# One attention kernel on one core: the shift of the scores summed by one matmul of stacked halves

## The reference

```python
q = jnp.einsum('bte,ef->btf', emb, Wq) + bq
k = jnp.einsum('bml,le->bme', latent, Wk) + bk
v = jnp.einsum('bml,le->bme', latent, Wv) + bv
w = jnp.einsum('bte,bme->btm', q, k) * scale        # scale = 1/sqrt(E)
w = jax.nn.softmax(w, axis=1)                       # over the tokens t
pred = jnp.einsum('btm,bme->bte', w, v)
x = pred + emb
return (x - mean(x)) * rsqrt(var(x) + EPS) * gamma + beta
```

## Time and profile before

| | |
|---|---|
| three runs | 143.15, 143.27 and 142.31 us, median 143.15 us |
| the profiled execution | 142.91 us |
| its span, first to last instruction | 141.2 us |
| mean granted TensorE clock | 0.994 of full speed |
| busy: TensorE, its weight loads, VectorE, ScalarE, GpSimd | 134.6, 130.4, 114.2, 79.0, 60.8 us |

### The profile page before, as it was taken

The page is one execution under the profiler, slowest core; times in us unless marked ns, Lnnn a source line. Parts: engine busy times, 40 slices in busy tenths (PEclk is TensorE's granted clock), DMA queues, the critical chain, the costliest instruction groups (busy, mean ns, idle before and its releaser), DMA issues.

```text
span 141.2 us, 2971 instructions
## 1 busy us (share of the span) xinstructions
PE 134.6 (95%) x1046; PEld 130.4 (92%) x1046; DVE 114.2 (81%) x221; ACT 79.0 (56%) x282; POOL 60.8 (43%) x61
## 2 busy tenths in 40 slices
PE   6999999999999999999999999999999999999940
PEld 6899999999998999999999999999999999999940
DVE  0479994996996769999999976878789976797983
ACT  4257088577276926466474829474747546386420
POOL 1000000027304590734848370629385644629791
PEclk9999999999999999999999999999999999999997
DMA  4999999956087495986998889796987987536314
GB/s 153 301 402 420 422 305 384 325 229 216 15 252 246 169 379 176 372 319 198 322 340 273 313 277 389 218 353 205 336 310 214 347 267 250 214 102 230 113 73 150
DMA packets 10814, 37.33 MB, mean 264 GB/s; under 512 B 1200, under 2 KB 1456, under 8 KB 10800
## 3 DMA queue, kind: packets, MB, share of 16 engines
q1 hardware_dynamic: 9424, 34.79, 71.0%
q10 hardware_dynamic: 1376, 2.36, 4.4%
HBM read 33.87 MB, written 3.28 MB: 263 GB/s over the span
## 4 chain that ended last, share of the span: by engine, by line
PE 89%; POOL 5%; issue 2%; ACT 1%; DVE 0%; POOLq 0%; DVEq 0%
PE ps_S L418 29%; PE ps_U L432 26%; PE ps_Y L453 10%; PE ps_U L391 6%; PE ps_Y L391 6%; POOL xT_in L971 3%; PE ps_Y L336 3%; POOL xT_in L959 2%; PE ps_w L441 1%; PE ps_S L340 1%; PE ps_U L498 1%; PE ps_c L406 1%; PE ps_U L340 1%; PE ps_c L407 1%; ACT xT_in L595 1%
## 5 line engine op out<-in xcount | busy, mean ns | idle before, releaser
L577 ACT ACTIVATE expo<-scores,negmax 121x100 f32<-121x100 f32 x96 | 35.0, 366 | 31.1 <-DVE negmax L746 31.1
L418 PE MATMUL ps_S<-G,ctxT_in 128*121 128x100 f32 (+1 forms) x384 | 43.4, 270 | 0.0
L418 PEld LDWEIGHTS ps_S<-G,ctxT_in 128*121 128x121 f32 (+1 forms) x384 | 42.1, 186 | 0.0
L432 PEld LDWEIGHTS ps_U<-prob,ctx_in 121*128 121x128 f32 x336 | 39.4, 192 | 0.9
L432 PE MATMUL ps_U<-prob,ctx_in 121*128 121x100 f32 x336 | 39.6, 275 | 0.0
L948 POOL TENSOR_TENSOR prob<-expo,rinv 121x600 f32<-121x600 f32 x16 | 19.2, 1203 | 30.8 <-DVE rinv L753 30.8
L959 POOL TENSOR_TENSOR xT_in<-x_in,xT_in 128x512 f32<-128x512 f32 (+1 forms) x13 | 17.0, 1314 | 19.8 <-issue 8.9
L742 DVE TENSOR_TENSOR scores<-ps_S,c_rows 121x600 f32<-121x600 f32 x16 | 12.5, 782 | 10.6 <-PE ps_S L418 7.5
L757 DVE TENSOR_REDUCE probsum<-prob 121x100 f32<-121x600 f32 x16 | 19.8, 1238 | 1.0 <-POOL prob L948 0.7
L577 ACT ACTIVATION_READ_ACCUMULATOR expo<-scores,negmax 121x1 f32 x96 | 18.0, 187 | 0.0
L964 POOL TENSOR_TENSOR rstd<-vareps,neg_half 128x1 f32<-128x1 f32 (+1 forms) x13 | 7.1, 548 | 23.2 <-DVE vareps L784 23.0
(11 more groups left out here) (122 smaller groups left out, 183.7 us busy)
## 6 DMA issues: line engine op xcount, KB each, us to landing
ctx_in<-ctx SPq DMA_DIRECT2D x16, 768.0 KB, 4.9
ctxT_in<-ctxT SPq DMA_DIRECT2D x16, 722.0 KB, 4.7
xT_in<-xT SPq DMA_DIRECT2D x8, 400.0 KB, 8.2
x_in<-x SPq DMA_DIRECT2D x12, 256.0 KB, 4.7
out<-xT_in ACTq DMA_DIRECT2D x8, 256.0 KB, 3.9
wqk<-Wqk SPq DMA_DIRECT2D x4, 388.0 KB, 4.6
out<-xT_in SPq DMA_DIRECT2D x3, 256.0 KB, 2.0
wv_in<-Wv SPq DMA_DIRECT2D x1, 512.0 KB, 16.3
```

Source lines behind the costliest of these rows:

```text
L418: last = nc.tensor.matmul(ps_scores(c)[0:rows(c), :], ctxT_in[:, q, l * M + c * MP:l * M + c * MP + rows(c)], G[:, l, bass.ds(b * T, T)], ...
L432: last = nc.tensor.matmul(ps_U[:, q, l * T:(l + 1) * T], ctx_in[0:rows(c), q, c, l * P:(l + 1) * P], prob[0:rows(c), q, c * T:(c + 1) * T] ...
L577: last = nc.scalar.activation(expo[0:MP, q, c * T:(c + 1) * T], scores[0:MP, q, c * T:(c + 1) * T], ACT.Exp, bias=negmax[0:MP, q, c:c + 1] ...
```

## The change

The four weighing steps stay. Behind the last of them VectorE adds the lower 64 partitions of `xu` to the upper 64 (a fold), so that 64 partial sums for each token are left. `upper_shift` writes their upper parts on partitions 0 to 63 of one array, `xu_parts`, and `lower_shift` their lower parts on partitions 64 to 127. So one matmul of ones over 128 partitions sums both. In group 0 the sum is made in four matmuls of 100 columns, one for each batch, and the copy to `c_rows` in two, the first batch alone, for which `maxima(0)` waits.

```diff
-        xu_hi = sb("xu_hi", [P, 2, GT], F32R)
-        xu_lo = sb("xu_lo", [P, 2, GT], F32R)
+        xu_parts = sb("xu_parts", [P, 2, GT], F32R)
...
+        PH = P // 2
...  sum_shift(g), TensorE
-                nc.tensor.matmul(ps_c[:, 0:GT], ones_r[:, :], xu_hi[:, g % 2, :], start=True, stop=False)
-                nc.tensor.matmul(ps_c[:, 0:GT], ones_r[:, :], xu_lo[:, g % 2, :], start=False, stop=True).then_inc(c_summed, 1)
+                if g == 0:
+                    for b in range(GB):
+                        last = nc.tensor.matmul(ps_c[:, b * T:(b + 1) * T], ones_r[:, :], xu_parts[:, 0, b * T:(b + 1) * T],
+                                                start=True, stop=True)
+                    last.then_inc(c_summed, 1)
+                else:
+                    nc.tensor.matmul(ps_c[:, 0:GT], ones_r[:, :], xu_parts[:, g % 2, :], start=True, stop=True).then_inc(c_summed, 1)
...  upper_shift(g), ScalarE
-                act.wait_ge(xu_step, EC * (g + 1))
+                act.wait_ge(xu_folded, g + 1)
                 if g >= 2:
                     act.wait_ge(c_summed, g - 1)
-                nc.scalar.activation(xu_hi[:, g % 2, :], xu[:, (EC - 1) % 2, :], ACT.Copy).then_inc(xuhi_set, 1)
+                nc.scalar.activation(xu_parts[0:PH, g % 2, :], xu[0:PH, 0, :], ACT.Copy).then_inc(xuhi_set, 1)
...  take_shift(g), ScalarE
-                nc.scalar.activation(c_rows[:, g * GT:(g + 1) * GT], ps_c[:, 0:GT], ACT.Copy).then_inc(c_set, 1)
+                if g == 0:
+                    nc.scalar.activation(c_rows[:, 0:T], ps_c[:, 0:T], ACT.Copy).then_inc(first_c_set, 1)
+                    nc.scalar.activation(c_rows[:, T:GT], ps_c[:, T:GT], ACT.Copy).then_inc(c_set, 1)
+                else:
+                    nc.scalar.activation(c_rows[:, g * GT:(g + 1) * GT], ps_c[:, 0:GT], ACT.Copy).then_inc(c_set, 1)
...  end of weigh_by_u(g), VectorE
+                if EC - 1 in terms:
+                    dve.wait_ge(xu_step, EC * (g + 1))
+                    nc.vector.tensor_tensor(xu[0:PH, 0, :], xu[0:PH, 1, :], xu[PH:P, 1, :], ALU.add).then_inc(xu_folded, 1)
+                    dve.wait_ge(xu_folded, g + 1)
...  lower_shift(g), VectorE
-                nc.vector.tensor_tensor(xu_lo[:, g % 2, :], xu[:, (EC - 1) % 2, :],
-                                        xu_hi[:, g % 2, :].bitcast(F32), ALU.subtract).then_inc(xulo_set, 1)
+                nc.vector.tensor_tensor(xu_parts[PH:P, g % 2, :], xu[0:PH, 0, :],
+                                        xu_parts[0:PH, g % 2, :].bitcast(F32), ALU.subtract).then_inc(xulo_set, 1)
...  maxima(b, q), VectorE
-                dve.wait_ge(c_set, b // GB + 1)
+                if b == 0:
+                    dve.wait_ge(first_c_set, 1)
+                else:
+                    dve.wait_ge(c_set, b // GB + 1)
```

More of the change, by code:

```diff
@@ L149, in xattn @@
         xu_step = sem("xu_step")
+        xu_folded = sem("xu_folded")
         xuhi_set = sem("xuhi_set")
@@ L155, in xattn @@
         c_set = sem("c_set")
+        first_c_set = sem("first_c_set")
         S_done = sem("S_done")
```

## The result

The changed kernel takes 148.12 us (median of six runs, 146.85 to 150.43) against 142.69 us (six runs of the kernel before): 1.0365 times as long, 95% interval 1.0322 to 1.0407. Forecast were 143.8 us and a range up to 145.0. One run of the six (150.43 us, lower granted clock) is left out of the ratio as disturbed.

What follows compares the result with a forecast made beforehand. TensorE, busy for 95% of the span, was taken to bound the kernel. Its lateness, 0 after group 1, -0.18 after group 2, +1.0 at 77 us, +0.82 from 93 us, gave 143.7, stated as 143.8 us; range 142.4 to 145.0.

Steps and rivals of the forecast that it cites:

- What TensorE could gain: TensorE, groups 0 to 3: up to 0.54 us saved in groups 1 to 3, group 0 0.05 dearer, net -0.49 us.
- The fold's 0.57 us: VectorE, each of four folds: an add of 400 elements takes 0.57 us, with waits 0.7 us, upper bound 1.1.
- the saved second matmul: TensorE, groups 1 to 3: one matmul of 400 columns goes, 0.18 to 0.19 us each.
- group 0 stayed within its bounds: Group 0: maxima(0) starts between 0.25 us earlier and 0.13 later; its matmuls 0.2 us dearer to 0.1 cheaper.
- the fold of group 3 inside the residual add: Near 75 us: GpSimd's add holds the fold until 76.99, TensorE goes on at 77.24 instead of 76.24, 1.0 us lost.
- Group 2 keeps its 0.18 us: TensorE after group 2: the 0.18 us saved by its matmul stays, so everything is 0.18 us early by 75 us.
- the alignment isn't chance: Group 3, near 75 us: the fold begins inside GpSimd's residual add, since that add and VectorE's variance step move together.
- the first thin place: Group 1, near 41 us: TensorE waits 0.2 us ahead of batch 3's scores and is at its old time, +-0.15.
- the sum: TensorE's lateness: 0 after group 1, -0.18 after group 2, +1.0 at 77 us, +0.82 us from 93 us on.
- held twice: Rival, group 3: GpSimd's next add goes first too, TensorE goes on 2.26 us late, end at 145.0 us; chance 0.12.

Runs made afterwards that it cites:

- the moved version: The changed kernel with the mask product on one column and the shift's work of groups 2 and 3 moved, group 2's steps moved again: 142.36 us, ratio 0.9969.
- the first experiment with the free product: The kernel before without its second shift matmul in groups 1 to 3, no fold, mask product on the last chunk's one column alone: 142.03 us, ratio 0.9955.
- the run with the filled gap: The changed kernel with ten matmuls more in TensorE's gap of 2.5 us ahead of the values of tile 4: 146.83 us, ratio 1.029.
- the one-column product: The changed kernel with the mask applied to the last chunk alone, one column times a per-partition scalar: 144.06 us, ratio 1.0084.

## Why the prediction was wrong, step by step

What TensorE could gain (0.49 us) was right within the noise: the moved version gives 0.37, and the first experiment with the free product 0.66 where 0.54 was to be had. The fold's 0.57 us and the saved second matmul were as forecast, and group 0 stayed within its bounds (the first maxima start at 24.71, 0.09 later than before). So was the step that was argued hardest, the fold of group 3 inside the residual add: alone it costs TensorE the 1.2 us that had been worked out, and the kernel 1.0 us once group 3's matmul is saved (143.91 against 142.87). The section "Who interferes with whom" of the Trainium skill's page "SBUF — State Buffer" holds here: a VectorE instruction with two SBUF operands (1.16, 1.52 and 1.73 us instead of 0.17, 0.57 and 0.63) waits for GpSimd, the one with a single column and a scalar (0.21) and `lower_U`, with an operand in PSUM, don't. The first weighing step, with one SBUF operand of 400 columns, is held too (1.49 us instead of 0.38).

The step that failed is "Group 2 keeps its 0.18 us", and with it the sentence that the alignment isn't chance because the residual add "follows VectorE's own variance step by a fixed queue, and both move together". The add follows the later of two things: VectorE's variance step, by way of the inverse deviation, and TensorE's `weight_sum`, by way of ScalarE. In the kernel before it is the second that comes last. Even the add at 75.07, of which the sentence spoke, started 0.20 us behind the end of the inverse deviation and 0.14 behind `value_bias`, which ended at 74.93; at 62.57 no inverse deviation stands ahead of the add in its turn. TensorE's 0.18 us moved the add, but not VectorE's product, which GpSimd had held back by way of the weighing step. At 62.6 us only 0.03 us lay between VectorE's product and GpSimd's add, and I had counted the product's holds without looking at those that it just escaped. Once it was held, VectorE was 1 us late, the weighing steps of group 3, harmless before, met the residual adds, and TensorE waited 1.22 us for the one and, with the fold's hold, 2.49 us for the other. In numbers of the profiled execution, on TensorE's chain: 0.37 late behind the first wait, 0.18 back, 1.22 + 0.20 for the first `values`, 2.49 + 0.20 for the second, 1.05 + 0.53 at the lower clock, 0.19 back. That makes 5.69 of the 5.73 us. Theory 1 has run in both directions: the saving without the folds brings the loss (145.07), the folds without the saving don't (143.87), and taking the product out of the way removes it in both kernels (144.06, 142.03).

Two smaller points. At the first thin place the sum had TensorE back at its old time, within 0.15 us, and the profiled execution has it 0.37 late behind it. That isn't a fixed price: in the run with the filled gap, the same kernel up to there, TensorE takes 8.43 us from the scores at 35.15 to the `values` at 43.58, and before 8.46 (35.17 to 43.63). In the profiled execution VectorE began with the shift 0.34 us later than before (18.33, 17.99), while TensorE was on time; with the filled gap it began at 17.81. The later two waits don't need this lateness: with the filled gap the product is held all the same (62.50, 1.14 us), and TensorE waits 1.22 us at 69.49. The fall of the clock wasn't in the sum at all; no row of the kernel before shows TensorE idle for long, so its price couldn't be read there. Of the rivals, "held twice" had the mechanism that came nearest, with the wrong instruction held first.

## What to carry to other kernels

A change that makes the busiest engine early isn't a pure gain if another engine's queue doesn't get early with it: list the pairs of instructions that share something (here a VectorE instruction with two SBUF operands and a GpSimd one), read the margin of each pair in the trace, those that just pass above all, and ask which of the two the change moves. Such a pair can be taken apart for nothing, as the one-column product was here. And what an engine gets back at one wait can be taken again by the next hold: VectorE had the 0.2 us at 57.70, and lost them behind a GpSimd product whose queue was still late.

## What the runs showed of the hardware

- A start in the profile that is a little earlier doesn't say which of the two is held. A weighing step that starts 0.02 us ahead of a GpSimd add is held by it (69.05 and 69.07; 68.50 and 68.52), one that starts 0.25 ahead isn't (67.99 and 68.24), and there the add takes 1.51 us instead of 1.28.
- A held VectorE instruction gets in between two GpSimd instructions that stand back to back, and the second then waits (1.59 to 1.63 us instead of 1.29), where the prediction had left it open.
- Behind TensorE's gap from 78.2 to 80.65 us the granted clock was 0.50 from about 81 to 84.4 us. With the gap filled the kernel took 146.83 us in place of 148.12, and the clock of that stretch was full. Behind waits of 1.23 us it was full as well.
- In the changed kernel `lower_shift`, whose output starts at partition 64, starts only behind the end of the product before it (35.84 against 35.64 + 0.17); in the kernel before it starts 0.08 us ahead of that end. This is what the Trainium skill's page "VectorE: DVE Perf Modes" states in its section "Two Vector instructions with no wait between them", and it is a part of the first wait: GpSimd's product beside it takes 1.51 us in place of 1.39, and holds the next weighing step by so much longer.
